# Attention stage of a macaron block: block transposes on VectorE, quotients on GpSimd, whole-tile splits, three score banks, and the next stage's first gates in the last turn

## The reference

```python
x = x + 0.5 * ffn(layernorm(x))       # 8 experts, the best 2 of each token, and a shared expert
x = x + attn(layernorm(x))            # below
x = x + 0.5 * ffn(layernorm(x))

def attn(x):                          # x: 32 sequences of 256 tokens, 128 features, 16 heads of 8
    Q, K, V = x @ W_Q.T, x @ W_K.T, x @ W_V.T
    attn = einsum('bhqd,bhkd->bhqk', Q, K) / sqrt(8)
    attn = where(causal, attn, -inf)
    probs = softmax(attn, axis=-1)
    return einsum('bhqk,bhkd->bhqd', probs, V) @ W_O.T
```

## Time and profile before

| | us |
|---|---|
| median of 3 runs | 1211.31 (1208.91 to 1214.98) |
| the profiled execution, its own time | 1214.04 |
| its span, first to last instruction | 1212.3 |
| its three stages in the span | 0 to 329.8, to 899.5, to 1212.3 |
| PE, DVE, ACT, POOL busy in the span | 1124.4, 1002.0, 789.4, 567.7 |

### The profile page before, as it was taken

One profiled execution on the slowest core, in us unless ns is written; L12 is line 12 of the kernel. 1 busy time (PEld: TensorE's weight loads), 2 busy tenths in 40 slices (PEclk: granted clock), 3 DMA queues, 4 the chain that ended last, 5 costly groups with the idle time before them and its releaser, 6 DMA issues. The chain is left out here.

```text
span 1212.3 us, 32050 instructions
## 1 busy us (share of the span) xinstructions
PE 1124.4 (93%) x11615; PEld 691.2 (57%) x11615; DVE 1002.0 (83%) x2583; ACT 789.4 (65%) x1545; POOL 567.7 (47%) x728
## 2 busy tenths in 40 slices
PE   3899999999989999999899999999978999999998
PEld 1566666666635555555555555555545666666665
DVE  4889999999657877888888788888758898998985
ACT  4676766767536665676676667676646667667664
POOL 2566666666603322333333223333325666666655
PEclk9899999999969998999999899999988999999999
DMA  4442443432200000000000000000004434435443
GB/s 125 153 159 90 149 144 101 136 129 85 70 1 2 2 2 1 2 2 2 2 2 2 2 2 2 2 1 2 2 2 141 145 101 151 126 114 158 117 122 97
DMA packets 59866, 80.13 MB, mean 66 GB/s; under 512 B 5568, under 2 KB 26944, under 8 KB 59712
## 3 DMA queue, kind: packets, MB, share of 16 engines
q1 hardware_dynamic: 59712, 78.08, 20.8%
HBM read 73.34 MB, written 4.72 MB: 64 GB/s over the span
## 5 line engine op out<-in xcount | busy, mean ns | idle before, releaser
L709 POOL TENSOR_TENSOR h_lo<-h,h_hi 128x512 f16<-128x512 f32 x288 | 333.5, 1158 | 233.9 <-ACT h_hi L656 231.8
L1167 DVE TENSOR_REDUCE neg_max_at<-score_at 128x2 f16<-128x512 f32 (+1 forms) x384 | 254.1, 691 | 80.1 <-PE score_at L993 74.9
L1282 POOL TENSOR_SCALAR_AFFINE_SELECT probs_at<-probs_at 128x512 f32<-128x512 f32 x256 | 156.3, 634 | 343.6 <-ACT probs_at L1241 343.6
L1241 ACT ACTIVATE probs_at<-prob_at 128x512 f32<-128x512 f32 x384 | 201.7, 599 | 77.3 <-PE prob_at L1025 75.2
L648 ACT ACTIVATE a<-a 128x512 f32<-128x512 f32 x256 | 149.0, 582 | 132.6 <-PE a L549 127.6
L435 DVE TENSOR_TENSOR prod<-a,gate_wide 128x512 f32<-128x512 f32 x256 | 176.0, 687 | 40.9 <-ACT a L648 40.1
L565 PE MATMUL y_b<-w_hi,h_hi 128*128 128x128 f16 x1152 | 207.8, 219 | 1.3 <-POOL h_lo L709 1.3
L565 PE MATMUL y_b<-w_lo,h_hi 128*128 128x128 f16 x1152 | 207.8, 219 | 0.0
L565 PE MATMUL y_b<-w_hi,h_lo 128*128 128x128 f16 x1152 | 207.8, 219 | 0.0
L656 ACT ACTIVATE h_hi<-h 128x512 f16<-128x512 f32 x288 | 179.5, 623 | 16.1 <-DVE h L445 15.5
L445 DVE TENSOR_TENSOR h<-prod,b 128x512 f32<-128x512 f32 x256 | 174.3, 681 | 4.9
(11 more groups left out here) (143 smaller groups left out, 1988.3 us busy)
## 6 DMA issues: line engine op xcount, KB each, us to landing
gate_wide<-gate_rows SPq DMA_DIRECT2D x256, 256.0 KB, 5.4
x<-in_L_attn_x_dram SPq DMA_DIRECT2D x16, 256.0 KB, 6.0
out_dram<-x SPq DMA_DIRECT2D x16, 256.0 KB, 6.9
raw_w<-in_L_ffn_w_dram SPq DMA_DIRECT2D x3, 512.0 KB, 5.3
gate_rows<-gate_rows SPq DMA_DIRECT2D x32, 16.0 KB, 1.4
raw_w<-in_L_ffn_sw_dram SPq DMA_DIRECT2D x3, 64.0 KB, 3.9
raw_attn<-in_L_attn_W_Q_dram SPq DMA_DIRECT2D x1, 64.0 KB, 4.8
raw_attn<-in_L_attn_W_K_dram SPq DMA_DIRECT2D x1, 64.0 KB, 3.0
```

What stands on the lines that cost most here:

```text
L709: nc.gpsimd.tensor_tensor(h_lo[k][:, :], h[k][:, :], h_hi[k][:, :], ALU.subtract).then_inc(hlo_done, 1)
L1167: nc.vector.tensor_reduce(dst, src, AX.X, ALU.max, negate=True).then_inc(max_done, 1)
L1241: nc.scalar.activation(probs[j % 2][:, i, :], prob_bank[i][:, :], ACT.Exp, scale=SCALE).then_inc(exp_done, 1)
L1282: nc.gpsimd.affine_select(out=p, in_=p, compare_op=ALU.is_ge, fill=0.0, base=0, pattern=[[0, GROUPS], [1, P]], channel_multiplier=-1).then ...
```

## The change

1. **Banks and thirds.** There are three score banks (one for each part) and two for transposed scores (part 2 uses part 0's). Part 2 of the transposed scores now comes behind weigh, interleaved with part 2 of the scores (thirds); ACT makes its exponent after the jobs of the first place.
2. **Block turns.** The jobs o and y, take_o, and PE's transposes in them are gone. o_bank gathers all four units of a sequence; DVE transposes it whole in blocks of 32 x 32 (128x512), POOL makes the inverse of 128x32 sums with a power of -1 and the product of 128x256 (quotient), DVE transposes the result in blocks (128x256), ACT makes the high part (split_y) and POOL the rest (low_y).
3. **Whole-tile splits.** q and k are split by one ACT and one DVE instruction each, 128x512. Each selection table becomes two (high and low), so that a Q or K job is four matmuls of 256 columns, not two. All Q jobs are taken by ACT. The table-building in the first stage (select_heads) has 10 parts instead of 16.
4. **Norm.** The scaling goes from DVE to ACT, with a shift that POOL makes; norm and root move to the turn's second unit.
5. **Next stage's first gates.** In the last turn PE makes the router product of the last stage's chunk 0, DVE its gates in 19 steps, ACT an exponent, and behind the last weigh PE transposes them, ACT takes them, SP stores and spreads them; the attention block ends only when these eight DMAs have landed. Chunk 0 of the last stage begins without them, and the 22 steps of chunk 1's gates are spread over it (GATE_PLACES_SECOND). The norm of the last stage's third chunk moves too. PE gets filler matmuls (keep_warm) there.
6. PLACES, SHIFT and the filler table WARM are new; q runs two turns ahead.

```diff
+GATE_PLACES_SECOND = (0, 0, 2, 2, 6, 8, 11, 14, 17, 20) + (GATE_STEPS,) * (2 * STEPS - 9)
...
-PLACES = (((), ("q",), ("k",)), (("o10",), ("o11",), ("Q00",)), (("K00",), ("Q01",), ("K01",)),
-          (("m10", "m11"), ("y1",), ()),
-          (("z1",), ("Q10",), ("K10",)), (("o00",), ("o01",), ("Q11",)), (("K11",), ("y0",), ("v",)),
-          (("m00", "m01"), ("x",), ("z0",)))
+PLACES = (((), ("k",), ("Q00",)), ((), (), ("K10", "K00")), (("K01", "Q01"), ("Q10",), ()),
+          (("m10", "m11"), ("v", "z1"), ()), ((), ("K11",), ()), ((), ("x", "Q11"), ()),
+          ((), (), ("z0",)), (("m00", "m01"), (), ("q",)))
...
-SHIFT = {n: -2 if n == "x" else -1 if n in ("m00", "m01") or n[0] in "qkQKv" else 1 if n in ("o10", "o11", "y1", "z1")
-         else 0 for n in JOBS}
-
-
-BESIDE_FIRST = [JOBS.index(n) for n in ("m10", "o00", "y0", "m00", "m00")]
+SHIFT = {n: -2 if n in "xq" else -1 if n in ("m00", "m01") or n[0] in "qkQKv" else 1 if n == "z1" else 0 for n in JOBS}
+BESIDE_FIRST = [JOBS.index(n) for n in ("Q10", "m11", "z1", "Q11", "m00")]
...
-WARM = {"Q00": 7, "K00": 3, "Q01": 1, "first": 4}
+WARM = {"q-": 5, "Q00": 2, "K10": 2, "first": 3}
+LAST_TURN = {"v": 2, "z1": 16}
...
-        score_bank = [bank(f"score{s}") for s in range(2)]
-        prob_bank = [bank(f"prob{i}") for i in range(3)]
+        score_bank = [bank(f"score{i}") for i in range(3)]
+        prob_bank = [bank(f"prob{s}") for s in range(2)]
...
+        @block.sync
+        def _(sp):
+
+            sp.wait_ge(next_rows, 1)
+            sp.dma_start(gating["dram"][0], gate_rows[:, :]).then_inc(next_stored, DMA)
+            sp.wait_ge(next_stored, DMA)
+            for e in range(EXPERTS):
+                spread_rows(sp, gating["dram"], gate_rows, [gating["wide0"]], 0, e).then_inc(next_loaded, DMA)
+            sp.wait_ge(next_loaded, EXPERTS * DMA)
 
...
-                        last = nc.tensor.matmul(tile, consts["sel_" + m][:, 2 * half + i, :],
-                                                stack[m][half][:, tokens], start=True, stop=True)
+                        for n, part in enumerate(("hi", "lo")):
+                            last = nc.tensor.matmul(tile, consts[f"sel_{m}_{part}"][:, 2 * half + i, :],
+                                                    split[m][n][:, tokens], start=(n == 0), stop=(n == 1))
...
-                wait_count(pe, max_done, n - 1)
-                dst = score_bank[(3 * j + i) % 2]
+                wait_count(pe, max_done, n - 2)
+                dst = score_bank[i]
...
-                wait_count(pe, exp_done, unit * 3 - 2 + i)
+                wait_count(pe, exp_done, unit * 3 + (0, -1, 1)[i])
...
+            def thirds(c, slot, b, j, ahead):
+                later, later_slot, later_b, later_j = ahead
+                part = begin_scores(later, later_b, later_j, 2)
+                begin_t(c, b, j, 2)
+                for h in range(GROUPS):
+                    head_t(slot, b, j, 2, h)
+                    if h % 2 == 1:
+                        score_head(later_slot, later_b, later_j, 2, part, h // 2)
...
-                wait_count(pe, o_done, unit)
+                if j == 0:
+                    wait_count(pe, o_step, (2 * c + b - 1) * O_STEPS + 1)
...
+            def next_turn():
...
+                            thirds(c, slot, b, j, ahead)
+                        else:
+                            scores_t(c, slot, b, j, parts=(2,))
                         turn_jobs(job, c, slot, places[1])
                         turn_jobs(job, c, slot, places[2])
+                        if c == CHUNKS - 1 and (b, j) == (0, 3):
+                            next_router()
...
+            keep_warm(LAST_TURN["v"])
             weigh(CHUNKS - 1, 1, 1, UNITS - 1)
-            turn_jobs(job, CHUNKS, 0, JOBS)
+            next_turn()
+            for name in JOBS:
+                keep_warm(LAST_TURN.get(name, 0))
+                turn_jobs(job, CHUNKS, 0, (name,))
...
-            def scale(c):
-
-                wait_taken(dve, c - 1, "x")
-                norm_scale(dve, nc, norm0 + c, chunk_rows(x, c), buf, ln_rooted, ln_done)
...
-                elif kind == "Q":
-
-                    wait_count(dve, st_done, (c - 1) * 6 * UNITS)
-                    last = nc.vector.tensor_copy(packed(q_pack[slot], name),
-                                                 src[:, :].rearrange("p (g n) -> p g n", n=SEQ))
+                    dve.wait_ge(qkhi_done, c * 2 + (1 if kind == "q" else 2))
+                    last = nc.vector.tensor_tensor(split[kind][1][:, :], src[:, :], split[kind][0][:, :], ALU.subtract)
...
+            def divide(c, b, step):
+
+                n = 2 * c + b
+                if step == 0:
+                    dve.wait_ge(pv_done, (n + 1) * UNITS)
+                    wait_count(dve, divided, n)
+                    done = nc.vector.transpose(o_rows[:, :, :, :].rearrange("p n i r -> p (n i r)"), o_bank[:, :])
+                else:
+                    dve.wait_ge(divided, n + 1)
+                    wait_count(dve, ylo_done, n)
+                    done = nc.vector.transpose(yt[:, :], y[:, :, :, :].rearrange("p s n r -> p n s r"))
+                done.then_inc(o_step, 1)
...
                         if ahead:
                             maxima(ahead[0], *ahead[2:], parts=(0, 1))
                         turn_jobs(job, c, slot, places[0])
+                        last_weighed(lambda *seq: divide(*seq, 0), c, b, j)
                         if ahead:
                             maxima(ahead[0], *ahead[2:], parts=(2,))
+                        last_weighed(lambda *seq: divide(*seq, 1), c, b, j - 1)
                         turn_jobs(job, c, slot, places[1])
-                        if b == 1 and j == 1:
+                        if (b, j) == (0, 1):
                             norm(c + 2)
-                        if b == 1 and j == 2:
-                            scale(c + 2)
                         turn_jobs(job, c, slot, places[2])
+                        if c == CHUNKS - 1 and b == 1:
+                            next_gates(*((0, 2), (2, 11), (11, NEXT_STEPS), (0, 0))[j])
+                            if j == 3:
+                                norm(CHUNKS + 2)
...
+                    nc.scalar.activation(split[kind][0][:, :], src[:, :], ACT.Copy).then_inc(qkhi_done, 1)
...
+            def scale(c, tiles):
+                act.wait_ge(shifted, 2 * (c - 2) + 2)
+                wait_taken(act, c - 1, "x")
+                for t in tiles:
+                    last = nc.scalar.activation(xn[:, t, :], chunk_rows(x, c)(t), ACT.Identity,
+                                                scale=buf["rstd"][:, t:t + 1], bias=buf["shift"][:, t:t + 1])
+                if t == TILES - 1:
+                    last.then_inc(ln_done, 1)
+
+            def split_y(c, b):
+                act.wait_ge(o_step, (2 * c + b + 1) * O_STEPS)
+                if b == 1:
+                nc.scalar.activation(yt_hi[:, :], yt[:, :], ACT.Copy).then_inc(yhi_done, 1)
...
-                        exponents(c, b, j)
+                        exponents(c, b, j, (0, 1))
                         places = PLACES[b * UNITS + j]
                         turn_jobs(job, c, slot, places[0])
-                        if j > 0:
+                        exponents(c, b, j, (2,))
                         turn_jobs(job, c, slot, places[1])
                         turn_jobs(job, c, slot, places[2])
+                        last_weighed(split_y, c, b, j - 1)
+                        if (b, j) == (0, 2):
+                            scale(c + 2, range(2))
+                        if (b, j) == (0, 3):
+                            scale(c + 2, range(2, TILES))
...
+            nc.scalar.activation(norms["table"][:, :], norms["eps"][:, 0:1], ACT.Silu)
+            next_take()
+            split_y(CHUNKS - 1, 1)
...
+            def quotient(c, b):
+                n = 2 * c + b
+                pool.wait_ge(o_step, n * O_STEPS + 1)
+                nc.gpsimd.tensor_tensor(inv[:, :, :], o_rows[:, :, :, HEAD], minus[:, :, :], ALU.pow).then_inc(inverted, 1)
+                pool.wait_ge(inverted, n + 1)
+                nc.gpsimd.tensor_tensor(y[:, :, :, :].rearrange("p s n (i d) -> p (s n) i d", d=HEAD),
+                                        o_rows[:, :, :, 0:HEAD],
+                                        inv[:, :, :].unsqueeze(3).to_broadcast([P, 2 * SEQ // ROWS, 2, HEAD]),
+                                        ALU.mult).then_inc(divided, 1)
+
+            def low_y(c, b):
+                pool.wait_ge(yhi_done, 2 * c + b + 1)
+                nc.gpsimd.tensor_tensor(yt_lo[:, :], yt[:, :], yt_hi[:, :], ALU.subtract).then_inc(ylo_done, 1)
...
                         mask(c, b, j)
-                        if b == 1 and j == 1:
+                        last_weighed(quotient, c, b, j)
+                        last_weighed(low_y, c, b, j - 1)
+                        if (b, j) == (0, 1):
```

(5 more changed lines are left out.)

423 lines of the change are left out of this document (232 added, 191 removed).

## The result

The changed kernel takes 1273.9 us (median of 4 runs, 1272.7 to 1275.5) against 1213.1 us for the kernel before on the same chip: 1.050 times as long, with a 95% interval of 1.047 to 1.053. The forecast of 1131 us and its range up to 1190 were wrong, and so was the sign. What came is rival A in its mechanism: the power on GpSimd has a price for each column.

The account below looks back on a forecast made before the run. PE's own work was taken to set the turn, with DVE close behind. From 1214.0 us, -77 for 16 turns and -3 at the ends gave 1134, or 1131 against the median; range 1100 to 1190.

Parts of the forecast that it names:

- rival A: GpSimd's power is priced per column: X is 6.8 us, a turn 38.2, the kernel about 1286; chance 0.13.
- X: Duration of GpSimd's power over 32 columns, inverting the row sums: between 1.1 and 6.8 us, taken as 1.5.
- thresholds 2.4 and 1.2: Values of X, in us, up to which GpSimd delays no weigh, in the first and second sequence.
- The clock: PE falling to its lower clock more often would make the forecast wrong; mean over attention 0.94, no cost given.
- The rest of the sum: A turn of attention: 33.3 less 3.7 of PE's list less 1.1 of waits, 28.5 us; 16 turns give -77.
- The list: PE's work in a turn: transposes -3.1, Q and K jobs +1.8, interleaved third parts -2.4; 3.7 us shorter.
- the four listed waits: PE's waits a turn: split by halves 0.53, maximum 0.65, Q copy 1.01, q_pack 0.34; all 2.5 us go.
- four small terms: Waits added to a turn: 0.5 and 0.4 through ACT, 0.3 through POOL's power, 0.2 from a denser list.
- the exponents' floor: Loop through ACT: the last exponent follows weigh, so a unit without jobs settles at 2.85 us, not 2.2.
- Thirds: On PE, part 2 of both scores interleaved takes 0.33 us instead of 0.31 + 0.32: -2.4 us a turn.
- rival C: The loop rules: third parts don't overlap or ACT's order holds every unit; turn about 31 us, 1171; chance 0.15.
- Ends: Expert 3 begins about 18 us after the last weigh, not 20.5: -3; attention's start and last tail cancel within 2.

Follow-up runs that it names:

- experiments 2 to 4: Changed kernel with the power over only 4 or 16 of 32 columns: 1102.2 and 1142.6 us; then powers of 4 to 64 columns on constants, in experiment 1's kernel.
- experiment 9: experiment 1's kernel with two score banks in turn instead of three: 1165.9 us, 0.962 of the kernel before.
- experiment 1: The changed kernel with the inverse of the row sums made by a VectorE reciprocal instead of GpSimd's power: 1101.4 us, 0.910 of the kernel before.

## Why the prediction was wrong, point by point

- **The failed step is X, the power's duration.** Between 1.1 and 6.8 the text took 1.5, on the ground that 0.207 us a column would be a hundred times an ordinary operation. The runs show 0.158 a column and 0.4 fixed (experiments 2 to 4): X = 5.45. The rule that the prediction named (the Trainium skill, GPSIMD Engine Reference, 2.1 Instruction dispatch) put the cost on the elements, and the measurement, 0.159 us for each further column from 8 to 64, agrees with it. A guess about what would be unusual stood against the only row on the operation, and the kernel before had a cheap measured way for the same values: its reciprocals, 0.248 us for 128x16, stood in the same trace.
- **What X does was right.** The thresholds 2.4 and 1.2 measured 2.7 to 2.9 and 1.4 (the text's own terms, 3.25 + 0.67 + 1.25, give 5.2 + X and not 5.3, and so 2.5 and 1.3). With X = 5.45 the text's own formula gives 28.2 + 3.05 + 4.25 = 35.5 us a turn and 1243 us in all: slower, but 31 us short of the truth. Rival A's 38.2 a turn and 1286 us lie near the measured 37.6 and 1274 through three errors that cancel: its power is too long (10.0 us of waits, measured 7.1), it has no clock in it (4.0 a turn), and its base is 1.7 us too high.
- **The clock** was named as a danger and not priced. Waits of 2.5 and 4.0 us cost another 4.0 us a turn; those of 0.2 and 1.5 cost 1.4 us in 4 of 14 turns.
- **The rest of the sum** gave 28.5 a turn, of it 0.3 for X; with a short power it is 26.48. Two terms were mis-sized, in opposite directions. The list shrank by 2.4, not 3.7: an o job took 0.49 and a y job 0.27 from start to start where nothing waited (below), so 2.5 left with the transposes and not 3.1; and thirds give 1.7 and not 2.4, since in the kernel before part 2 followed the heads of parts 0 and 1 directly (0.76 for both the earlier trace rows), while now the heads, with a table, weigh or a job behind them, take 0.54 (509.68 to 510.22) and the thirds 0.33 (508.58 to 508.91). The Q and K jobs grew by 0.22 each, as forecast. Rows of the kernel before on the two jobs and what follows each:

```profile
613.32 0.44 PE L949 MATMUL job_at<-ident,y_at 128*128 128x128 f32 x2
613.59 0.38 PE L983 MATMUL score_at<-causal,ident_b 128*128 128x512 bf16 x1
...
620.78 0.66 PE L940 MATMUL job_at<-ident,o_t_at 128*128 128x128 f32 x4
621.27 0.38 PE L926 MATMUL job_at<-q_stack_at,sel_q 128*128 128x256 f16 x2
```

- **The waits** that went were more than the 2.5 read from the listed ones. Units of 20.1 and jobs of 8.5 (from start to start, where nothing waits) make a pure list of 28.6 of the 33.3 us; 4.7 was waiting, of which the profile marks 2.9 (the four listed waits and one of 0.33 for a maximum); the rest lay in gaps that stretched a record or were too short to be marked. After the change with a short power 0.3 is left. Which parts removed them is shown for the third bank alone (experiment 9): the whole-tile splits, the Q copies on ScalarE, the norm's move and the new job table were not taken apart. The four small terms that the text added, 1.4 in all, came to about nothing: the exponents' floor exists (2.88 against 2.85 forecast), but the one unit seen at it has 0.44 of jobs and was nearly as long anyway. Also not in the sum: the kernel before had, beside its turns of 33.3, some of 34.4 and 37.1 us with a lower clock (x jobs at 628.85, 663.30 and 700.37), and experiment 1 has none between its second and its last turn.
- **Thirds** overlap as forecast (0.33 for the pair); rival C did not occur.
- **VectorE and ScalarE**: 23.7 and 21.9 us a turn, forecast 23 to 25 and about 22. A mask takes 636 ns (634 before), and no single one more than 647, so the block transposes, which overlap some of them by 0.4 us, don't hold GpSimd up, as expected.
- **Ends.** With experiment 1's kernel, timelines of TensorE and of the queues (expert 3's first matmul is the one at 797.27):

```profile
777.78 1.51 PE L1113 MATMUL o_at<-probs_at,v_ones_at 128*32 128x256 f32 x16 [0.52 <-POOL probs_at L1398]
...
797.27 0.38 PE L568 MATMUL a<-xt_hi,w_hi 128*128 128x512 f16 x1
```

```profile
779.94 0.32 SPq L885 DMA_DIRECT2D gate_rows<-gate_rows  x1
781.34 3.84 SPq L298 DMA_DIRECT2D gate_wide<-gate_rows  x8
```

  Weigh ends at 779.3, expert 3 begins 18.0 us later, as forecast. By the same measure the kernel before takes 19.9 (893.02 + 1.39 = 894.4 to 914.34); the forecast's 20.5 took that weigh as short as at full clock. From there to the end it takes 299.5 us, before 298.0: 1.5 of the 1.9 is given back. Nor does the tail of the last turn cancel as forecast: TensorE's clock is 0.50 in it from 767.5 to past the last weigh, in the kernel before only around the last two weighs (0.50 in 892 to 893). No experiment took this part alone.

## What to carry to other kernels

An operation whose price is seen at one size only has two prices, fixed and per element, and the range must be carried through to the sign of the result; if one end turns the sign, the operation stays where it is measured to be cheap. Here the whole change was worth 9% with a VectorE reciprocal of 0.35 us and cost 5% with a GpSimd power of 5.45 us. Waits should be read as the turn less the pure list from start to start, not as the sum of the marked ones.
